# Key products, query products, context sums and the output projection take new places among the attention's steps

## The chip, the cores and the metric

The kernel runs on one core of a Trainium2 chip. The metric is device time in microseconds (us) of one execution. TensorE is called PE here, VectorE DVE, ScalarE ACT, GpSimd POOL and SyncE SP, as in the profile.

## The reference

Three layers follow each other on 4 sequences of 256 tokens with 256 features: half a mixture-of-experts layer, an attention layer, and the same mixture-of-experts layer again, each on layer-normalised input and added to it.

```python
x = x + 0.5 * ffn(layernorm(x))
x = x + attn(layernorm(x))      # the layer that the change is in
x = x + 0.5 * ffn(layernorm(x))

def attn(inputs, w_q, w_k, w_v, w_o, b_o):       # 16 heads of 16 features, t = 256
    q, k, v = ((inputs @ w.T).reshape(b, t, 16, 16) for w in (w_q, w_k, w_v))
    scores = einsum("bqhd,bkhd->bhqk", q, k)     # causal
    attn = softmax(where(causal, -inf, scores) / sqrt(t))
    ctx = einsum("bhqk,bkhd->bqhd", attn, v).reshape(b, t, 256)
    return ctx @ w_o.T + b_o
```

## The kernel before

The feed-forward layers are not touched. Only the attention is of interest, some 120 us between them.

**Steps.** A sequence (`b`, 0 to 3; called a batch) has 8 head pairs, and `sweep` runs 8 steps for each, s = 0 to 7, then 5 more at the end (b = 4, only old work). Every engine runs its own `step(b, old, new)` in program order, and semaphores tie the engines together. The scores of a pair are made `SLAG` = 2 steps after the batch's step 0, so the last two pairs of a batch are scored in steps 0 and 1 of the next. A pair's scores are a "tail" (second 128 queries by 256 keys, bank 0 or 1) and a "head" (first 128 queries by 128 keys, bank 2 or 3).

**A plain step.** PE: `scores` tail, `scores` head, then `weigh` of the pair three steps back. `scores` needs the pair's masked keys from POOL (`mask_keys`, four operations on `k_head`, which has two slots) and, for its bank, DVE's `low` of two pairs before. DVE: tail maximum (L1200), `low` tail of the previous pair (L1214), head maximum (L1204), `low` head (L1214). ACT: `high` of the previous pair (L834, L837), tail exponentials (two L812, each with a read of the accumulator), head exponentials (two L819). When `low` head is done, SP starts the transposition of the pair's probabilities by DMA into `pT` (L446), and `weigh` (L1596 to L1598) of two steps later on waits for it.

**Extra work in some steps.** `chunk(b, c)` makes 128 of the 256 columns of query and of key with 8 matmul records (L1547) in bank 7: query in its left half, key in its right. It stands in steps 0 and 3 (`CHUNK_STEP`), on PE between tail and head scores. ACT copies it out rounded (`k_hi` L798, `q_hi` L799, which shares the memory named xT_hi), between tail and head exponentials. DVE makes the remainders (`k_lo` L1187, `q_lo` L1189) between head maximum and `low` head. The masks of steps 2 to 5 use key chunk 0, those of steps 6, 7 and the next 0, 1 use key chunk 1.

Step 5 (`SUM_STEP`): DVE's `add_up` waits for all weighing of the batch before, reduces banks 5 and 6 to `ctxv` (L1222 twice) and takes the reciprocal (L1224), all ahead of its tail maximum. PE's `weigh` of step 5 writes the same two banks anew, so it waits for both reductions:

```python
if s == SLAG + 3:
    if old:
        pe.wait_ge(ctx_summed, b * 2)
```

Step 6 (`OUT_STEP`): POOL divides `ctxv` (L388, after its masks of step 6); PE transposes it into bank 7 (L1610) between tail and head scores; ACT copies it out as `ctxT` (L844, stored in the memory named wv) ahead of its `high`. Step 7: PE projects (`project_out`, L1617, 8 matmul records, bank 7) ahead of its tail scores, and DVE adds the result to x (`add_attention`, L1229) at the end of the step. `chunk` of the next step 0 waits for that (`attn_added`).

Of the kernel before, what the change touches and what calls it, by code (L numbers as in the profile page):

```python
# [56 lines left out]
P_SCALE = 2.0 ** 15  # L57
VBANK = (3, 4, 5, 6, 5, 6, 5, 6)
VALUES = {1: (0, 2), 2: (2, 4), 3: (4, 6), 4: (6, 8)}
# [4 lines left out]
OBANK = (7, 4)  # L64
CHUNK_STEP = (0, 3)
SUM_STEP, OUT_STEP = 5, 6
# [13 lines left out]
def build(nc, x_in, wq_in, wk_in, wv_in, wo_in, bo_in, wr_in, win_in, wout_in, bias_in, out):  # L80
    with ExitStack() as ctx:
# [241 lines left out]
        v_ready = sem("v_ready")  # L323
        qk_done = sem("qk_done")
        qk_hi_ready = sem("qk_hi_ready")
        k_hi_ready = sem("k_hi_ready")
        k_lo_ready = sem("k_lo_ready")
        qk_ready = sem("qk_ready")
        k_head_ready = sem("k_head_ready")
# [49 lines left out]
        def steps_of(new):  # L379

            return range(HPAIRS if new else SUM_STEP)

# [264 lines left out]
        def _(act):  # L647
# [145 lines left out]

            def chunk(b, c):

                act.wait_ge(qk_done, b * DK + (c + 1))
                reach(act, head_scored, b * HPAIRS + (CPAIRS * (c + 1) - HPAIRS))
                act.activation(k_hi[:, c, :], bank[7][:, SEQ:2 * SEQ], ACT.Copy).then_inc(k_hi_ready, 1)  # L798
                act.activation(q_hi[c][:, :, :], bank[7][:, 0:SEQ].rearrange("p (q t) -> p q t", q=2), ACT.Copy,  # L799
                               scale=1.0 / SEQ ** 0.5).then_inc(qk_hi_ready, 1)  # L800

# [37 lines left out]

            def step(b, old, new):  # L840
                for s in steps_of(new):
                    if old and s == OUT_STEP:
                        act.wait_ge(ctxT_done, b)
                        act.activation(ctxT[:, :, :], bank[7][:, :].rearrange("p (k t) -> p k t", k=DK), ACT.Copy,  # L844
                                       scale=1.0 / P_SCALE).then_inc(ctxT_ready, 1)
                    if old if s < SLAG + 1 else new:
                        high(b, s)
                    if old if s < SLAG else new:
                        exps(b, s, True)
                    if not old and s == 0:  # L850
                        turn_out(1, (1,))
                    if new and s in CHUNK_STEP:
                        chunk(b, CHUNK_STEP.index(s))
# [36 lines left out]
        def _(dve):  # L890
# [292 lines left out]

            def chunk(b, c):

                dve.wait_ge(qk_hi_ready, b * DK + (c + 1))
                dve.tensor_tensor(k_lo[:, c, :], bank[7][:, SEQ:2 * SEQ], k_hi[:, c, :].bitcast(F32), ALU.subtract)\  # L1187
                    .then_inc(k_lo_ready, 1)
                dve.scalar_tensor_tensor(q_lo[c][:, :, :], bank[7][:, 0:SEQ].rearrange("p (q t) -> p q t", q=2),  # L1189
                                         1.0 / SEQ ** 0.5, q_hi[c][:, :, :].bitcast(F32),  # L1190
                                         ALU.mult, ALU.subtract).then_inc(qk_ready, 1)

# [23 lines left out]

            def add_up(b):

                sums = row_sum[:, bass.ds(b - 1, 1), :, :].rearrange("p o q h -> p (o q) h")
                dve.wait_ge(pv_done, b * HEADS)  # L1220
                for qt in range(2):
                    dve.tensor_reduce(ctxv[:, qt, :, :], bank[5 + qt][:, :].rearrange("p (h w d) -> p h d w", w=2, d=HD),  # L1222
                                      AX_X, ALU.add).then_inc(ctx_summed, 1)
                dve.reciprocal(inv_sum[:, :, :], sums).then_inc(inv_ready, 1)  # L1224

            def add_attention(b):
                dve.wait_ge(o_done, b)
                rows = x[:, bass.ds(b * 2 - 2, 2), :]
                dve.tensor_tensor(rows, rows, bank[7][:, :].rearrange("p (q d) -> p q d", q=2), ALU.add)\  # L1229
                    .then_inc(attn_added, 1)  # L1230
# [17 lines left out]
            def step(b, old, new):  # L1248
                for s in steps_of(new):
                    if old and s == SUM_STEP:  # L1250
                        add_up(b)
                    if old if s < SLAG else new:
                        maxima(b, s, True)
                    if old if s < SLAG + 1 else new:
                        low(b, s, True)
                    if old if s < SLAG else new:
                        maxima(b, s, False)
                    if new and s in CHUNK_STEP:
                        chunk(b, CHUNK_STEP.index(s))
# [65 lines left out]
        def _(pe):  # L1325
# [211 lines left out]

            def chunk(b, c):

                if c:  # L1540
                    pe.wait_ge(qk_ready, b * DK + c)
                else:

                    reach(pe, attn_added, b)
                for w, to in ((wq, 0), (wk, SEQ)):
                    for k in range(DK):
                        last = pe.matmul(bank[7][:, to:to + SEQ], w[:, k, c * P:(c + 1) * P], xnT[:, k, bass.ds(b * SEQ, SEQ)],  # L1547
                                         start=(k == 0), stop=(k == DK - 1))
                last.then_inc(qk_done, 1)

            def values(first, last):
                for t in range(first, last):

                    reach(pe, v_rest_ready, t - 1 if t >= 4 else 0)
                    for k in range(DK):
# [4 lines left out]
            def scores(b, s, tail):  # L1560
# [5 lines left out]
                if tail:  # L1566
                    if (s - SLAG) % CPAIRS == 0:

                        pe.wait_ge(qk_ready, b * DK + (c + 1 - (DK if s < SLAG else 0)))
                    pe.wait_ge(k_head_ready, g + 1)  # L1570
# [13 lines left out]
            def weigh(b, s):  # L1584

                g = b * HPAIRS + (s - SLAG - 3)
                ago = s < SLAG + 3
                turned = pT[(s - 1) % 2]
                pe.wait_ge(pT_ready[g % 2], g // 2 * 16 + 16)
# [11 lines left out]
            def turn_context(b, new):  # L1601

                pe.wait_ge(ctx_ready, b)
                if new:

                    pe.wait_ge(qk_ready, b * DK + DK)
                for c in range(DK):
                    for qt in range(2):
                        heads = ctxv[:, qt, c * HPC:(c + 1) * HPC, :].rearrange("p h d -> p (h d)")
                        last = pe.transpose(bank[7][:, c * SEQ + qt * P:c * SEQ + (qt + 1) * P], heads, ident[:, :])  # L1610
                last.then_inc(ctxT_done, 1)

            def project_out(b):
                pe.wait_ge(ctxT_ready, b)
                for qt in range(2):
                    for c in range(DK):
                        last = pe.matmul(bank[7][:, qt * D:(qt + 1) * D], ctxT[:, c, qt * P:(qt + 1) * P], wo[:, c, :],  # L1617
                                         start=(c == 0), stop=(c == DK - 1))
                last.then_inc(o_done, 1)

            def step(b, old, new):
                for s in steps_of(new):
                    if old and s == OUT_STEP + 1:
                        project_out(b)
                    if old if s < SLAG else new:
# [9 lines left out]
                    if new and s in CHUNK_STEP:  # L1635
                        chunk(b, CHUNK_STEP.index(s))
                    if not old and s == SLAG + 1:
# [4 lines left out]
                    if old if s < SLAG + 3 else new:  # L1642
                        if s == SLAG + 3:
# [84 lines left out]
```

## Time and profile before

| | |
|---|---|
| time, median of 3 runs | 421.43 us (420.86 to 422.84) |
| the profiled execution | 420.87 us, its span 419.1 us |
| mean granted TensorE clock | 0.990 |
| busy share of the span | PE 91%, DVE 71%, ACT 61%, POOL 57% |
| step 0 of batch 1 to step 0 of batch 4 | 77.69 us, in three batches of 25.02, 25.40 and 27.27 us |

The span runs from the first to the last instruction; 1.8 us of the profiled execution lie around it. Busy shares are means over stages with different limits, so the attention has to be read by itself. There the start of each tail maximum (DVE L1200) is a clock of the steps: exactly one begins in every step.

### The profile page before, as it was taken

To read this page: it belongs to the slowest core of one execution; us is meant where nothing else is said; L and a number is where in the kernel's file an instruction comes from. 1 tells how busy PE (TensorE), PEld (TensorE's weight loads), DVE (VectorE), ACT (ScalarE), POOL (GpSimd) and SP (SyncE) were. 2 spreads that over 40 slices of the span, in tenths; PEclk is the share of its full clock that TensorE was granted. 3 is DMA by queue.
4 is the path that set the end of the run, shared out by engine and by line. 5 is a ranking of instruction groups with operands and counts; after the bars stand their busy time and mean duration, and the time that the engine had idled before them with its cause. 6 is when DMAs were issued, how large, how long until landed. Compare 5 with 4: busy or idle time off the path is not lost.

```text
span 419.1 us, 9185 instructions
## 1 busy us (share of the span) xinstructions
PE 380.4 (91%) x2732; PEld 309.0 (74%) x2733; DVE 296.6 (71%) x620; ACT 256.6 (61%) x640; POOL 237.5 (57%) x307
## 2 busy tenths in 40 slices
PE   7769999999999989788888988797899999999996
PEld 3548888888888867566666766473788888888885
DVE  6878999555666796887777757967466765566566
ACT  2837865656555546799888878621455556555552
POOL 5255445565567359567878668201555545745860
PEclk9999999999999999899999989999999999999999
DMA  7949921112111620466867587819721111112126
GB/s 253 399 125 391 379 97 54 52 38 75 50 50 38 238 77 0 76 114 116 151 117 129 103 108 145 139 20 305 238 96 55 53 62 52 50 50 57 43 96 231
DMA packets 70929, 51.57 MB, mean 123 GB/s; under 512 B 53104, under 2 KB 64624, under 8 KB 70640
## 3 DMA queue, kind: packets, MB, share of 16 engines
q1 hardware_dynamic: 66064, 36.99, 34.3%
q0 software_dynamic: 4544, 12.07, 9.3%
q10 hardware_dynamic: 288, 2.10, 1.3%
q8 instruction: 17, 0.28, 0.3%
q14 instruction: 16, 0.13, 0.1%
HBM read 29.37 MB, written 9.19 MB: 92 GB/s over the span
## 4 chain that ended last, share of the span: by engine, by line
PE 57%; DMA 16%; DVE 15%; issue 4%; ACT 3%; POOL 2%; SPq 1%; DVEq 0%; ACTq 0%; POOLq 0%
PE bank L1408 27%; PE bank L1430 13%; DMA pT<-parts 5%; DMA w_raw<-in_win_t 4%; PE bank L1418 4%; PE bank L1580 3%; DMA pT<-parts_late 3%; PE bank L1547 3%; PE bank L1384 2%; DMA w_out<-y_scratch 2%; DVE x L1097 2%; DMA y_scratch<-arena,scatter_row 2%; DVE neg_max L1200 1%; PE bank L1617 1%; DVE parts L1214 1%
## 5 line engine op out<-in xcount | busy, mean ns | idle before, releaser
L546 POOL DMA_INDIRECT arena<-xn_scratch,gather_row x46 | 49.6, 1078 | 68.1 <-PE bank L1384 46.7
L552 POOL DMA_INDIRECT y_scratch<-arena,scatter_row x42 | 62.5, 1488 | 37.1 <-ACT arena L715 35.3
L1408 PE MATMUL bank<-w_hi,xT_hi 128*128 x184 | 61.7, 416 | 0.4 <-ACT xT_hi L674 0.4
L1058 DVE TENSOR_TENSOR wo_lo<-w_out,wo_hi 128x1024 fp32r<-128x1024 f32 x46 | 56.3, 1224 | 3.8 <-PE bank L1430 2.2
L1063 DVE TENSOR_TENSOR gT_lo<-bank,gT_hi 128x512 fp32r<-128x512 f32 x46 | 31.7, 690 | 38.1 <-ACT gT_hi L689 38.1
L1408 PE MATMUL bank<-w_hi,xT_lo 128*128 x184 | 57.5, 393 | 0.0
L1408 PE MATMUL bank<-w_lo,xT_hi 128*128 x184 | 57.3, 392 | 0.0
L682 ACT ACTIVATE arena<-bank 128x512 f32<-128x512 f32 x46 | 27.6, 599 | 45.6 <-PE bank L1408 45.6
L627 POOL TENSOR_TENSOR k_head<-k_hi,head_mask 128x256 fp32r<-128x256 f32 x64 | 38.7, 626 | 24.3 <-PE bank L1581 24.3
L704 ACT ACTIVATE wo_hi<-w_out 128x1024 fp32r x46 | 48.8, 1061 | 5.1 <-issue 3.0
L1580 PE MATMUL bank<-k_head,xT_hi 128*128 128x256 f32 (+1 forms) x128 | 40.2, 395 | 7.7 <-DVE parts L1214 5.9
L1047 DVE TENSOR_TENSOR xT_lo<-bank,xT_hi 128x256 fp32r<-128x256 f32 x46 | 19.5, 425 | 34.8 <-ACT xT_hi L674 34.4
L1408 PEld LDWEIGHTS bank<-w_lo,xT_hi 128*128 128x128 f32 x184 | 34.5, 188 | 8.1
L1408 PEld LDWEIGHTS bank<-w_hi,xT_lo 128*128 128x128 f32 x184 | 34.5, 188 | 7.9
L715 ACT ACTIVATE arena<-bank 128x256 f32<-128x256 f32 x42 | 16.2, 386 | 37.2 <-PE bank L1430 37.2
L627 POOL TENSOR_TENSOR k_head<-k_lo,head_mask 128x256 fp32r<-128x256 f32 x64 | 38.0, 614 | 0.6 <-DVE k_lo L1187 0.6
L812 ACT ACTIVATE bank<-bank,neg_max 128x256 f32<-128x256 f32 x64 | 28.5, 446 | 12.4 <-DVE neg_max L1200 11.7
L1430 PE MATMUL bank<-wo_hi,gT_hi 128*128 128x256 f32 x184 | 33.0, 301 | 1.4 <-ACT gT_hi L689 1.4
L1329 PE MATMUL bank<-ones 128*128 128x512 f16 x108 | 28.4, 395 | 4.8 <-POOL ident L496 1.8
L1072 DVE TENSOR_TENSOR arena<-arena,bank 128x512 f32<-128x512 f32 x46 | 31.2, 678 | 1.1 <-PE bank L1408 0.9
L1200 DVE TENSOR_REDUCE neg_max<-bank 128x2 f32<-128x512 f32 x32 | 21.9, 684 | 13.0 <-PE bank L1581 13.0
L1430 PE MATMUL bank<-wo_hi,gT_lo 128*128 128x256 f32 x184 | 30.1, 286 | 0.6 <-DVE gT_lo L1063 0.5
(196 smaller groups left out, 915.5 us busy)
## 6 DMA issues: line engine op xcount, KB each, us to landing
w_raw<-in_win_t SPq DMA_DIRECT2D x8, 1024.0 KB, 10.9
w_out<-in_wout_t SPq DMA_DIRECT2D x16, 512.0 KB, 7.6
w_out<-y_scratch SPq DMA_DIRECT2D x8, 512.0 KB, 5.3
xn_scratch<-arena ACTq DMA_DIRECT2D x2, 1024.0 KB, 6.2
x<-in_x SPq DMA_DIRECT2D x4, 256.0 KB, 3.4
out<-x SPq DMA_DIRECT2D x4, 256.0 KB, 2.2
arena<-xn_scratch,gather_row POOLq DMA_INDIRECT x46, 3.4
y_scratch<-arena,scatter_row POOLq DMA_INDIRECT x46, 3.0
```

The costliest lines, as they stand in the source:

```text
L546: pool.indirect_dma_start(out=xb[j % 2][:, :], out_offset=None, in_=xn_dram, in_offset=bass.IndirectOffsetOnAxis(ap=gather_row[:, j:j + 1] ...
L552: pool.indirect_dma_start(out=y_dram, in_=y[j % 2][:, :], in_offset=None, out_offset=bass.IndirectOffsetOnAxis(ap=scatter_row[:, j:j + 1], ...
L627: ins = pool.tensor_tensor(k_head[s % KSLOTS][:, part, hh, :], k[:, c, :].bitcast(F32), head_mask[:, h % HPC:h % HPC + 1].to_broadcast([P, ...
L704: act.activation(wo_hi[u][:, :, :], w_out[:, bass.ds(e, 1), :, :].rearrange("p o c d -> p (o c) d"), ACT.Copy)\
L812: act.activation(keys, keys, ACT.Exp, bias=neg_max[u][:, 1, hh:hh + 1], accum_out=row_sum[:, bass.ds(batch, 1), 1, h:h + 1]).then_inc(tail ...
L1058: dve.tensor_tensor(wo_lo[:, :, :], w_out[:, bass.ds(e, 1), :, :].rearrange("p o c d -> p (o c) d"), wo_hi[u][:, :, :].bitcast(F32), ALU.s ...
L1063: dve.tensor_tensor(gT_lo[:, :, :], bank[4][:, :].rearrange("p (c t) -> p c t", c=HK), gT_hi[:, :, :].bitcast(F32), ALU.subtract).then_inc ...
L1072: dve.tensor_tensor(g[:, :], sa[:, :], bank[2 + u][:, :], ALU.mult).then_inc(g_done, 1)
L1329: pe.matmul(bank[into][:, :], ones[:, :], bc(ones[:, :], 1, [P, 512 // P, P]), start=True, stop=True)
L1408: last = pe.matmul(bank[2 * half + u][:, :], tok[u][:, k, :], wts[:, bass.ds(e, 1), k, half * H:(half + 1) * H], start=(part == 0 and k == ...
L1430: last = pe.matmul(bank[y_bank(j)][:, 0:D], tok[:, c, :], wts[:, c, :], start=(part == 0 and c == 0), stop=(part == 2 and c == HK - 1))
L1580: pe.matmul(to, q[:, 1 if tail else 0, :], keys[:, part, :, 0:width], start=(n == 0), stop=False)
```

## The change

- Query and key get banks of their own (query bank 4, key bank 7) and are made apart: key chunk 0 of the next batch in step 6, query chunk 0 in step 0, key chunk 1 in step 3, query chunk 1 in step 4. In the very first batch key chunk 0 is made in step 0. The last batch has no next one and makes none in step 6.
- The context sum: one of the two reductions stays ahead of step 5's tail maximum, the other goes between `low` tail and head maximum of step 5. The reciprocal goes to the end of step 4.
- The transposition of the context goes behind `weigh` in step 6, its copy on ACT behind the head exponentials; both use bank 4.
- The projection goes in two halves: one between tail and head scores of step 7, one behind its `weigh`.
- The value products of the first batch leave bank 4 (`VBANK`). `weigh` and its wait stay where they are.

```diff
-VBANK = (3, 4, 5, 6, 5, 6, 5, 6)
+VBANK = (3, 5, 6, 5, 6, 5, 6, 5)
-CHUNK_STEP = (0, 3)
+KEY_STEP, QUERY_STEP = (6, 3), (0, 4)
 # ACT, step
-                    if old and s == OUT_STEP:
-                        act.wait_ge(ctxT_done, b)
-                        act.activation(ctxT[:, :, :], bank[7][:, :].rearrange("p (k t) -> p k t", k=DK), ACT.Copy,
-                                       scale=1.0 / P_SCALE).then_inc(ctxT_ready, 1)
                     if old if s < SLAG + 1 else new:
                         high(b, s)
                     if old if s < SLAG else new:
                         exps(b, s, True)
...
+                    if new and s == KEY_STEP[0] and b + 1 < BATCH:
+                        key_chunk(b + 1, 0)
+                    if new and s == KEY_STEP[1]:
+                        key_chunk(b, 1)
+                    if new and s in QUERY_STEP:
+                        query_chunk(b, QUERY_STEP.index(s))
                     if old if s < SLAG else new:
                         exps(b, s, False)
+                    if old and s == OUT_STEP:
+                        act.wait_ge(ctxT_done, b)
+                        act.activation(ctxT[:, :, :], bank[4][:, :].rearrange("p (k t) -> p k t", k=DK), ACT.Copy,
+                                       scale=1.0 / P_SCALE).then_inc(ctxT_ready, 1)
 # DVE, step
-                    if old and s == SUM_STEP:
-                        add_up(b)
+                    if old and new and s == SUM_STEP:
+                        add_up(b, 0)
                     if old if s < SLAG else new:
                         maxima(b, s, True)
                     if old if s < SLAG + 1 else new:
                         low(b, s, True)
+                    if old and new and s == SUM_STEP:
+                        add_up(b, 1)
                     if old if s < SLAG else new:
                         maxima(b, s, False)
...
                     if old if s < SLAG + 1 else new:
                         low(b, s, False)
+                    if old and new and s == SUM_STEP - 1:
+                        invert(b)
 # PE, step
-                    if old and s == OUT_STEP + 1:
-                        project_out(b)
                     if old if s < SLAG else new:
                         scores(b, s, True)
-                    if old and s == OUT_STEP:
-                        turn_context(b, new)
...
+                    if old and new and s == OUT_STEP + 1:
+                        project_out(b, 0)
...
                         weigh(b, s)
+                    if old and new and s == OUT_STEP + 1:
+                        project_out(b, 1)
+                    if old and new and s == OUT_STEP:
+                        turn_context(b, new)
```

The chunk functions are the old one cut in two, with a semaphore for each product; on PE:

```python
def key_chunk(b, c):
    reach(pe, k_lo_ready, b * DK + c)
    ...                                   # 2 matmuls into bank 7, then k_done
def query_chunk(b, c):
    reach(pe, q_ready, b * DK + c)
    if c == 0:
        reach(pe, attn_added, b)
    ...                                   # 2 matmuls into bank 4, then q_done
```

## Rows read from the trace of the kernel before

**Rows 1.** By stretch: us, then PE, PEld, DVE, ACT, POOL busy, clock, DMA, GB/s.
```profile
185.01:210.03 25.02, 21.77 (x236) 16.92 (x234) 18.96 (x40) 21.94 (x86) 19.63 (x35) 1.00 0.71 128
210.03:235.43 25.40, 22.00 (x236) 17.24 (x236) 18.98 (x42) 21.96 (x86) 19.64 (x35) 1.00 0.72 126
235.43:262.70 27.27, 23.35 (x238) 18.38 (x239) 18.97 (x41) 21.96 (x86) 19.62 (x35) 0.94 0.71 117
```

**Rows 2.** Timeline of ACT in batch 2: start, duration, work.
```profile
212.13 0.38 ACT L798 ACTIVATE k_hi<-bank 128x256 fp32r<-128x256 f32 x1 [0.35 <-PE bank L1547]
212.41 0.38 ACT L799 ACTIVATE xT_hi<-bank 128x256 fp32r<-128x256 f32 x1
...
216.32 0.59 ACT L834 ACTIVATE parts<-bank 128x512 f16<-128x512 f32 x1
...
217.23 0.45 ACT L812 ACTIVATE bank<-bank,neg_max 128x256 f32<-128x256 f32 x1
...
218.16 0.34 ACT L819 ACTIVATE bank<-bank,neg_max 128x128 f32<-128x128 f32 x1
...
218.86 0.60 ACT L834 ACTIVATE parts_late<-bank 128x512 f16<-128x512 f32 x1
...
229.33 0.60 ACT L844 ACTIVATE wv<-bank 128x512 f32<-128x512 f32 x1 [0.51 <-PE bank L1610]
```

**Rows 3.** Timeline of DVE in batch 2, steps 0 to 7.
```profile
213.28 0.42 DVE L1189 SCALAR_TENSOR_TENSOR xT_lo<-bank,xT_hi 128x256 fp32r<-128x256 f32 x1
213.62 0.41 DVE L1214 SCALAR_TENSOR_TENSOR parts_late<-bank,parts_late 128x256 f16<-128x256 f32 x1
...
216.50 0.69 DVE L1200 TENSOR_REDUCE neg_max<-bank 128x2 f32<-128x512 f32 x1 [0.58 <-PE bank L1581]
...
217.71 0.41 DVE L1204 TENSOR_REDUCE neg_max<-bank 128x2 f32<-128x256 f32 x1
...
219.55 0.69 DVE L1200 TENSOR_REDUCE neg_max<-bank 128x2 f32<-128x512 f32 x1 [1.09 <-PE bank L1581]
...
223.10 0.69 DVE L1200 TENSOR_REDUCE neg_max<-bank 128x2 f32<-128x512 f32 x1
...
224.97 1.28 DVE L1222 TENSOR_REDUCE ctxv<-bank 128x256 f32<-128x512 f32 x2
226.17 0.34 DVE L1224 RECIPROCAL inv_sum<-placed 128x32 f32<-128x32 f32 x1
226.43 0.63 DVE L1200 TENSOR_REDUCE neg_max<-bank 128x2 f32<-128x512 f32 x1
...
232.89 0.69 DVE L1200 TENSOR_REDUCE neg_max<-bank 128x2 f32<-128x512 f32 x1 [1.09 <-PE bank L1581]
```

**Rows 4.** The chain that ended last, in order of time, at step 2.
```profile
214.06 3.88 DMA pT<-parts_late
```

**Rows 5.** Timeline of PE in batch 2, steps 3, 6 and 7.
```profile
218.44 0.71 PE L1580 MATMUL bank<-k_head,xT_hi 128*128 128x512 f32 x2
...
219.35 1.03 PE L1547 MATMUL bank<-arena,wq 128*128 128x256 f32 x4
220.22 1.03 PE L1547 MATMUL bank<-arena,wk 128*128 128x256 f32 x4
220.89 0.59 PE L1580 MATMUL bank<-k_head,xT_hi 128*128 128x256 f32 x2
...
222.01 0.48 PE L1580 MATMUL bank<-k_head,xT_hi 128*128 128x512 f32 x1
...
230.06 1.97 PE L1617 MATMUL bank<-wo,wv 128*128 128x256 f32 x8
231.69 0.58 PE L1580 MATMUL bank<-k_head,xT_hi 128*128 128x512 f32 x1
```

**Rows 6.** The same columns as rows 1, around step 3 of batch 3.
```profile
242.00:243.00 1.00, 0.33 (x3) 0.10 (x1) 1.00 (x2) 0.96 (x4) 1.00 (x3) 1.00 1.04 194
...
244.00:245.00 1.00, 1.00 (x20) 0.90 (x21) 0.00 (x0) 1.00 (x5) 0.96 (x2) 0.50 0.70 154
```

More of the change, by code:

```diff
@@ L379, in steps_of @@
         def steps_of(new):
-            return range(HPAIRS if new else SUM_STEP)
+            return range(HPAIRS if new else SLAG + 3)
         def divide(eng, b):
@@ L1255, in step @@
                         low(b, s, True)
+                    if old and new and s == SUM_STEP:
+                        add_up(b, 1)
                     if old if s < SLAG else new:
                         maxima(b, s, False)
[L1258 to L1259 removed]
+                    if not old and s == 0:
+                        key_chunk(0, 0)
+                    if new and s == KEY_STEP[0] and b + 1 < BATCH:
+                        key_chunk(b + 1, 0)
+                    if new and s == KEY_STEP[1]:
+                        key_chunk(b, 1)
+                    if new and s in QUERY_STEP:
+                        query_chunk(b, QUERY_STEP.index(s))
                     if old if s < SLAG + 1 else new:
                         low(b, s, False)
+                    if old and new and s == SUM_STEP - 1:
+                        invert(b)
                     if not new and s == 0:
@@ L1536, in _, with key_chunk, query_chunk @@
             pe.wait_ge(xnT_ready, TPAIRS + 1)
[L1538 to L1542, printed above, removed]
-                    reach(pe, attn_added, b)
[L1545 to L1549, printed above, removed]
+            def key_chunk(b, c):
+                reach(pe, k_lo_ready, b * DK + c)
+                for k in range(DK):
+                    last = pe.matmul(bank[7][:, 0:SEQ], wk[:, k, c * P:(c + 1) * P], xnT[:, k, b * SEQ:(b + 1) * SEQ],
+                                     start=(k == 0), stop=(k == DK - 1))
+                last.then_inc(k_done, 1)
+            def query_chunk(b, c):
+                reach(pe, q_ready, b * DK + c)
+                if c == 0:
+                    reach(pe, attn_added, b)
+                for k in range(DK):
+                    last = pe.matmul(bank[4][:, 0:SEQ], wq[:, k, c * P:(c + 1) * P], xnT[:, k, b * SEQ:(b + 1) * SEQ],
+                                     start=(k == 0), stop=(k == DK - 1))
+                last.then_inc(q_done, 1)
             def values(first, last):
                 for t in range(first, last):
-                    reach(pe, v_rest_ready, t - 1 if t >= 4 else 0)
+                    reach(pe, v_rest_ready, t - 1 if t >= 3 else 0)
                     for k in range(DK):
@@ L1609, in turn_context, with project_out @@
                         heads = ctxv[:, qt, c * HPC:(c + 1) * HPC, :].rearrange("p h d -> p (h d)")
-                        last = pe.transpose(bank[7][:, c * SEQ + qt * P:c * SEQ + (qt + 1) * P], heads, ident[:, :])
+                        last = pe.transpose(bank[4][:, c * SEQ + qt * P:c * SEQ + (qt + 1) * P], heads, ident[:, :])
                 last.then_inc(ctxT_done, 1)
-            def project_out(b):
+            def project_out(b, qt):
                 pe.wait_ge(ctxT_ready, b)
[L1615 to L1619, printed above, removed]
+                for c in range(DK):
+                    last = pe.matmul(bank[4][:, qt * D:(qt + 1) * D], ctxT[:, c, qt * P:(qt + 1) * P], wo[:, c, :],
+                                     start=(c == 0), stop=(c == DK - 1))
+                if qt:
+                    last.then_inc(o_done, 1)
             def step(b, old, new):
                 for s in steps_of(new):
-                    if old and s == OUT_STEP + 1:
-                        project_out(b)
                     if old if s < SLAG else new:
@@ L1632, in step @@
                         turn(2, (0,))
-                    if old and s == OUT_STEP:
-                        turn_context(b, new)
-                    if new and s in CHUNK_STEP:
-                        chunk(b, CHUNK_STEP.index(s))
+                    if not old and s == 0:
+                        key_chunk(0, 0)
+                    if new and s == KEY_STEP[0] and b + 1 < BATCH:
+                        key_chunk(b + 1, 0)
+                    if new and s == KEY_STEP[1]:
+                        key_chunk(b, 1)
+                    if new and s in QUERY_STEP:
+                        query_chunk(b, QUERY_STEP.index(s))
+                    if old and new and s == OUT_STEP + 1:
+                        project_out(b, 0)
                     if not old and s == SLAG + 1:
```

58 lines of the change are left out of this document (32 added, 26 removed).

## Prediction

> **What bounds the kernel now.** I read the busy time of each engine by stretch first. A batch of attention takes 25.02, 25.40 and 27.27 us, and ACT is busy for 21.94 to 21.96 us of each, DVE for 19, POOL for 19.6 [rows 1]. PE's 22 us are partly pipeline. So no engine is full: at most 25.40 - 21.96 = 3.4 us a batch is waiting, some 10 us over three batches, and that is all that a new order could win.
>
> The timelines come next, with the start of each tail maximum as T. ACT without a gap needs 0.91 us for two `high` copies, 0.93 for the tail and 0.70 for the head exponentials, 2.54 us a step [rows 2]. Step 2 starts at 216.50, step 3 at 219.55, step 4 at 223.10, step 5 at 226.43, step 7 at 232.89 [rows 3], and batch 2 itself runs from 210.03 to 235.43 [rows 1]. Against 2.54 a step, steps 0 to 3 take 9.52 for 7.62, step 3 to 4 3.55, step 4 to 5 3.33, and steps 5 to 0 take 9.00 for 7.62. The reader should see that each loss stands beside an extra job: chunk, sum, projection.
>
> The chain tells what the chunk of step 0 does. `low` head of step 0 starts at 213.62, 3.59 us after T0 [rows 3]. Its transposition lands at 214.06 + 3.88 = 217.94 [rows 4], `weigh` of step 2 waits for it, and T3 comes 1.61 later. So from a late `low` head to the tail maximum three steps on it is 4.32 + 1.61 = 5.93 us. In a plain step `low` head starts 1.21 + 0.33 = 1.54 after T (217.71 less 216.50, and the 0.34 between two such operations), and 1.54 + 5.93 = 7.47 hides under ACT's 7.62: the two are nearly tied.
>
> **Prices used.** From T to the tail exponentials 0.73 (217.23 less 216.50); a hand-over between engines 0.04 (the maximum ends at 217.19, ACT starts at 217.23); one rounded copy costs ACT 0.28 and takes 0.38 [rows 2, 3]. A remainder costs DVE 0.34, `low` head 0.34, a reduction 0.60 to the next and 0.68 to its end (1.28 less 0.60), the reciprocal 0.26 [rows 3]. On PE: tail scores 0.91 up to a product, 1.11 up to T; one product 0.87 when first and 0.67 when second; head scores and `weigh` together 1.12 (220.89 to 222.01); the projection 1.63, so 0.82 a half; tail scores behind a projection 1.20 up to T (231.69 to 232.89) [rows 3, 5].
>
> **The change, part by part, in a batch.**
>
> *Steps 0 to 3.* PE holds one product instead of two, but what is late now is the remainder of the query: it waits for ACT's copy, which stands behind the tail exponentials. `low` head starts at 0.73 + 0.93 + 0.38 + 0.04 + 0.34 = 2.42 after T0 instead of 3.59. T3 = 2.42 + 5.93 = 8.35 instead of 9.52: 1.17 won. ACT alone would allow 7.62 + 0.28 = 7.90.
>
> *Step 3 to 4.* PE: 0.91 + 0.87 + 1.12 = 2.90; DVE 2.42 + 0.34 = 2.76; ACT 2.54 + 0.28 = 2.82. PE ends last: 2.90 instead of 3.55, 0.65 won. With the product at 0.67 it is ACT's 2.82.
>
> *Step 4 to 5.* Before, step 4 had no chunk. Now DVE waits for the query's rounded copy, so `low` head starts at 2.42, ends its turn at 2.76, then the reciprocal 0.26 and the first reduction 0.60: 3.62 instead of 3.33, 0.29 lost. Behind DVE's wait stand the reduction and the maximum, and ACT waits for the latter.
>
> *Step 5 to 6.* `weigh` still waits for both reductions, and the second has been put behind the tail maximum. It starts at T5 + 1.21, ends at 1.89, and after `weigh` and the tail scores T6 is at 1.89 + 1.61 = 3.50. This is the cost that moving half the sum does not show by itself: before, both reductions were over ahead of T5 and hid under DVE's own time. Behind the waiting `weigh` on PE stand the tail scores of step 6, and everything waits for these.
>
> *Step 6 to the next 0.* The copy of the context stands behind the head exponentials: 0.73 + 0.93 + 0.28 + 0.70 = 2.64 after T6. It takes 0.60, and PE's projection follows 0.13 later (229.93 to 230.06), at 3.37 [rows 2, 5]. First half 0.82, head scores and `weigh` 1.12, second half 0.82, then 1.20 to the tail maximum: 3.37 + 0.82 + 1.12 + 0.82 + 1.20 = 7.33. The tail scores of step 7 fit in the wait ahead of the first half. Cutting the projection in two removes no PE work; its second half stands squarely ahead of the next step's tail scores. Steps 5 to 0 so take 3.50 + 7.33 = 10.83 instead of 9.00: 1.83 lost. The second half starts at T6 + 5.31 and is over at about 6.3; adding the attention to x (512 columns on DVE, 0.69 as the tail maximum of the same size) ends at about 7.0, before T0, and the query product, due at 6.13 + 0.91 = 7.04, does not wait for it.
>
> *At no cost.* POOL's 32 mask and 2 divide operations of a batch take 19.64 us [rows 1], 0.58 each. The two divides can only start at T5 + 1.9 and take some 1.2; the mask of step 7 then ends at about T5 + 5.4 (four operations, 2.3 us), and PE wants it at T6 + 2.1 = T5 + 5.6. It is covered by 0.2 us; without the cover, each 0.1 late is 0.1 on T7. The number of transpositions and SP's order don't change. The key chunk of step 6 is ready long before masks need it.
>
> *Sum of a batch.* 8.35 + 2.90 + 3.62 + 3.50 + 7.33 = 25.70, against 25.02, 25.40 and, in batch 3, 25.40 plus a clock dip of 1.87. Batch 3 has no key chunk in step 6 and takes 25.42. So +0.68, +0.30, +0.02: +1.0 us. Batch 0 gives one copy (0.28) out of step 3 and takes one into step 4 and one into step 6: +0.3, with value work around it that can hide or double this (0 to 0.6). Together +1.3 us on 420.87 = 422.2. This execution is 0.56 under the median of 421.43, so I forecast 422.7. The unknown bounds (product 0.67 or 0.87, ties between engines of 0.1 to 0.2 a step) make it 0.3 us a batch either way, 421.5 to 424.
>
> **TensorE's clock.** In batch 3, PE had 0.33 us of work in one us, then little, and at 244 the granted clock was 0.50 (1.2 GHz) while PE was fully busy with what had waited [rows 6]. That stretch cost 27.27 - 25.40 = 1.87 us. I read it as the wait of `weigh` on a late transposition, since step 0 has its chunk in this batch too. The changed kernel has a wait of that kind in each batch: head scores of step 5 can start when `low` head of step 4 is done, at T5 - 0.86, and take less than the 1.12 that they need with `weigh`. So PE has no work from T5 + 0.3 at the latest to T5 + 1.9, for 1.6 to 2.7 us.
>
> The Trainium skill ("TensorE: Matmul & The Clock Gate", section "HAM oscillation") warns that gaps in which the matmul engine idles between bursts bring its clock down, so that the burst behind each gap runs slow. By that rule, if it struck in every batch, the sum would be 422.7 + 2 x 1.87 = 426.4. The trace agrees as far as rows 6 go; that batches 1 and 2 kept full clock shows it doesn't strike every time.
>
> **The rivals.**
>
> *A, one dip more or three dips instead of one.* For it: the new wait in step 5. Against it: before, similar waits in other batches left the clock at 1.00 [rows 1]. One more is 424.6, two more 426.4. Chance 0.30 in all, 0.20 and 0.10.
>
> *B, the dip of batch 3 goes.* The late transposition that led to it is 1.17 earlier. Then 422.7 - 1.9 = 420.8. Chance 0.15.
>
> *C, faster.* One mechanism: PE's held `weigh` in step 5 doesn't pace steps 5 to 0, ACT does. It decides at the point where `weigh` can start by T5 + 1.66, when ACT ends the tail exponentials. Then these steps take 3 x 2.54 + 0.28 for the key copy + 0.60 for the context's = 8.50 instead of 10.83, and the kernel 422.7 - 3 x 2.33 = 415.7. For it: ACT has the most work of the three others [rows 1]. Against: the wait stays in the code and its end is DVE's, T5 + 1.89 at the earliest. Chance 0.10, half of it only part of the way, around 418.5.
>
> *D, the change does less than it says.* POOL's masks wait for free slots rather than for keys, and wins and losses shrink together: 421.4, chance 0.05.
>
> My forecast itself has 0.40.
>
> **How the numbers follow.** No change that can be measured here is within 0.5% (419.3 to 423.5). It gets D and B, and of the forecast three quarters (its part up to 423.5): 0.05 + 0.15 + 0.30 = 0.50. Slower gets A and the rest of the forecast: 0.30 + 0.10 = 0.40. Faster is C, 0.10. The range goes from 419.3, which leaves most of C out, to 426.0, which leaves the last tenth of A out. The forecast's own range is 421.5 to 424.
>
> **What the new profile would show.** `low` head of step 0 some 2.4 us after the tail maximum, not 3.6; steps 0 to 3 in about 8.4 us. The tail maximum of step 5 3.6 after that of step 4. In step 5, the second reduction behind the first `low`, PE idle until it ends, and 3.5 us to step 6. Between the halves of the projection no long wait, and 7.3 us from step 6 to the next step 0. ACT busy for 22 us a batch as before. I am wrong if `weigh` of step 5 is not the one that PE waits on, if batches take under 25.2 us at full clock, or if the clock falls more than once after step 0 of batch 1.

## The result and the profile after

The changed kernel takes 424.05 us, median of 10 runs (421.92 to 425.06), against 421.45 for the kernel before (10 runs, 419.69 to 422.84). The ratio is 1.0071, with a 95% interval of 1.0048 to 1.0094: 0.7% slower. The profiled execution took 424.78 us, its span 423.0 us against 419.1, its mean granted clock 0.976 against 0.990. Of the kernels built later, both_whole and sum_alone had three runs each over 1.5% above their fastest; the ratios, medians and low-clock times below leave those out, and the profile of both_whole is one of them.

The stretches of batches 1, 2 and 3 come first, from tail maximum to tail maximum of step 0, with the columns of [rows 1].

```profile
188.18:214.84 26.66, 23.12 (x236) 17.77 (x235) 19.49 (x40) 22.43 (x87) 19.89 (x35) 0.94 0.68 122
214.84:240.99 26.15, 23.01 (x236) 18.20 (x237) 19.58 (x40) 21.99 (x85) 19.71 (x35) 0.93 0.67 122
240.99:266.55 25.56, 21.02 (x234) 16.54 (x235) 19.16 (x39) 21.50 (x84) 19.68 (x35) 1.00 0.68 125
```

The loss of this one execution adds up over the span. Up to the first tail maximum it is 0.41 us (161.75 for 161.34), in batch 0 (to its successor's step 0) 2.76 (26.43 for 23.67), in batch 1 1.64, in batch 2 0.75, in batch 3 a gain of 1.71, and behind it 0.05 (156.45 for 156.40): 3.90, the difference of the spans. The clock column matters: batches 1 and 2 now run partly at half speed (0.94 and 0.93), and batch 3, which did so before, no longer does. In batch 0 the clock is 0.87 on average, against 0.93 before.

DVE's timeline of batch 2, with L1216 the tail maximum, L1206 the query's remainder, L1238 the reciprocal and L1243 the two reductions, answers to [rows 3]:

```profile
214.84 0.69 DVE L1216 TENSOR_REDUCE neg_max<-bank 128x2 f32<-128x512 f32 x1
...
217.24 0.41 DVE L1230 SCALAR_TENSOR_TENSOR parts_late<-bank,parts_late 128x256 f16<-128x256 f32 x1
...
223.01 0.69 DVE L1216 TENSOR_REDUCE neg_max<-bank 128x2 f32<-128x512 f32 x1 [0.69 <-PE bank L1617]
...
225.74 0.68 DVE L1216 TENSOR_REDUCE neg_max<-bank 128x2 f32<-128x512 f32 x1
...
227.79 0.42 DVE L1206 SCALAR_TENSOR_TENSOR xT_lo<-bank,xT_hi 128x256 fp32r<-128x256 f32 x1 [0.30 <-ACT xT_hi L805]
...
228.46 0.34 DVE L1238 RECIPROCAL inv_sum<-placed 128x32 f32<-128x32 f32 x1
228.72 0.63 DVE L1243 TENSOR_REDUCE ctxv<-bank 128x256 f32<-128x512 f32 x1
229.26 0.68 DVE L1216 TENSOR_REDUCE neg_max<-bank 128x2 f32<-128x512 f32 x1
...
230.45 0.68 DVE L1243 TENSOR_REDUCE ctxv<-bank 128x256 f32<-128x512 f32 x1
...
232.76 0.69 DVE L1216 TENSOR_REDUCE neg_max<-bank 128x2 f32<-128x512 f32 x1 [0.96 <-PE bank L1617]
```

`low` head of step 0 starts 2.40 us after the tail maximum instead of 3.59, and steps 0 to 3 take 8.17 instead of 9.52. Step 3 to 4 takes 2.73 instead of 3.55. In step 4 DVE waits 0.30 for ACT's query copy, and step 4 to 5 takes 3.52 instead of 3.33. The second reduction ends at 230.45 + 0.68 = 231.13, and step 5 to 6 takes 3.50 instead of 2.47.

The waits of the same stretch name it on PE (total, times, longest), once for its weights and once for its matmuls:

```profile
PEld bank L1632 <- DVE ctxv L1243: 2.0, 1, 2.0
PE bank L1632 <- DVE ctxv L1243: 1.9, 1, 1.9
```

And the stretches around that wait, with the clock as the first number behind POOL:

```profile
228.00:231.00 3.00, 1.12 (x7) 0.60 (x5) 3.00 (x7) 2.23 (x9) 1.44 (x3) 1.00 0.80 154
231.00:234.00 3.00, 2.81 (x27) 2.21 (x28) 2.04 (x5) 2.08 (x9) 2.72 (x5) 0.81 0.57 108
234.00:237.00 3.00, 3.00 (x31) 2.52 (x29) 1.14 (x4) 2.12 (x10) 2.63 (x6) 0.62 0.36 67
```

PE works 1.12 of 3 us, then has everything to do that had waited, and does part of it at half speed: 2.4 falls to 1.2 GHz. To be set beside [rows 5], from PE's timeline: the one key product of step 6, four records, takes 1.62 us there; four such records took 1.03.

```profile
232.56 1.62 PE L1572 MATMUL bank<-arena,wk 128*128 128x256 f32 x4
```

### The profile page after: what moved, and what is told of

It is laid out like the page before. It is cut to its first block, busy times and chain, and to the rows that moved or that the text cites. A ratio compares the mean times of both kernels' runs of the same rounds, so it can differ in the third digit from the quotient of the medians.

```text
span 423.0 us, 9196 instructions
## 1 busy us (share of the span) xinstructions
PE 386.1 (91%) x2732; PEld 312.0 (74%) x2733; DVE 298.7 (71%) x620; ACT 256.6 (61%) x640; POOL 237.2 (56%) x307
## 4 chain that ended last, share of the span: by engine, by line
PE 64%; DVE 15%; DMA 8%; issue 6%; ACT 5%; POOL 2%; DVEq 1%; ACTq 0%; SPq 0%; POOLq 0%
PE bank L1438 27%; PE bank L1460 13%; PE bank L1616 4%; PE bank L1448 4%; PE bank L1359 3%; DMA pT<-parts 3%; PE bank L1414 2%; ACT bank L818 2%; DVE w_lo L942 2%; DMA arena<-xn_scratch,gather_row 2%; DVE neg_max L1216 2%; DMA w_out<-y_scratch 2%; PE bank L1652 1%; DVE v L1314 1%; DVE parts L1230 1%
## 5 line engine op out<-in xcount | busy, mean ns | idle before, releaser
L1616 PE MATMUL bank<-k_head,xT_hi 128*128 128x256 f32 (+1 forms) x128 | 42.7, 416 | 8.4 <-DVE parts L1230 6.3
L1359 PE MATMUL bank<-ones 128*128 128x512 f16 x108 | 32.1, 436 | 3.5 <-POOL ident L497 1.8
L1216 DVE TENSOR_REDUCE neg_max<-bank 128x2 f32<-128x512 f32 x32 | 22.0, 687 | 14.5 <-PE bank L1617 14.1
L1616 PEld LDWEIGHTS bank<-k_head,xT_hi 128*128 128x128 f32 x128 | 22.3, 201 | 12.8 <-issue 7.5
```

Of the source, the lines that this page charges most:

```text
L1359: pe.matmul(bank[into][:, :], ones[:, :], bc(ones[:, :], 1, [P, 512 // P, P]), start=True, stop=True)
L1616: pe.matmul(to, q[:, 1 if tail else 0, :], keys[:, part, :, 0:width], start=(n == 0), stop=False)
```

## The experiments

All were compared with the kernel before on the same chip. Beside the ratio, two readings are used. The first is the distance between tail maxima in one profile. The second is the low-clock time of a run: a run of span s and mean granted clock c has 2 x (1 - c) x s us at half clock. For the 84 runs of the kernel before that came with the experiments it is 9.4 us on average; for the 10 runs of the changed kernel 17.3. In the profiles this time comes in low stretches of 3.4 us each, or of 6.8.

| kernel | median, us | ratio (95%) | low clock, us | steps 0-3, 3-5, 5-6, 6-0 in batch 2 |
|---|---|---|---|---|
| before | 421.4 to 421.6 | 1 | 9.4 | 9.52, 6.88, 2.47, 6.53 |
| changed | 424.05 | 1.0071 (1.0048 to 1.0094) | 17.3 | 8.17, 6.25, 3.50, 8.23 |
| sum_whole | 422.43 | 1.0021 (0.9990 to 1.0052) | 12.8 | 8.15, 6.84, 2.52, 7.13 |
| out_whole | 425.77 | 1.0125 (1.0082 to 1.0168) | 23.1 | 8.20, 6.25, 3.49, 7.43 |
| both_whole | 422.00 | 0.9996 (0.9966 to 1.0027) | 12.3 | 8.20, 6.84, 2.77, 8.79 |
| filled | 425.25 | 1.0077 (1.0048 to 1.0106) | 13.0 | 8.32, 6.25, 3.49, 7.13 |
| sum_query_early | 418.40 | 0.9933 (0.9906 to 0.9959) | 10.0 | 8.28, 5.98, 2.92, 7.12 |
| filled_all | 430.92 | 1.0248 (1.0215 to 1.0280) | 23.5 | 10.28, 7.41, 3.50, 7.13 |
| before_filled | 431.33 | 1.0237 (1.0191 to 1.0284) | 18.3 | 11.81, 7.46, 2.46, 6.65 |
| sum_query_filled | 421.36 | 1.0015 (0.9989 to 1.0041) | 9.6 | 9.62, 5.98, 2.91, 7.14 |
| sum_alone | 424.03 | 1.0065 (1.0027 to 1.0102) | 14.5 | 9.51, 6.24, 3.49, 6.57 |
| out_alone | 421.04 | 1.0002 (0.9979 to 1.0025) | 7.4 | 9.34, 6.88, 2.46, 6.87 |
| first_query_3 | 423.82 | 1.0061 (1.0029 to 1.0093) | 19.4 | 8.23, 6.25, 3.69, 8.27 |
| best_first_3 | 418.78 | 0.9928 (0.9900 to 0.9957) | 11.5 | 8.25, 5.97, 2.88, 7.13 |

**One part undone: sum_whole.**

```diff
 # DVE, step of the changed kernel
                     if old and new and s == SUM_STEP:
                         add_up(b, 0)
+                        add_up(b, 1)
                     if old if s < SLAG else new:
                         maxima(b, s, True)
                     if old if s < SLAG + 1 else new:
                         low(b, s, True)
-                    if old and new and s == SUM_STEP:
-                        add_up(b, 1)
```

> The changed kernel, but both reductions of the context sum stand ahead of the tail maximum of step 5 again (the reciprocal stays at the end of step 4). Theory 1, the held weighing is the cost: steps 4 to 5 grow from 3.52 by one reduction, 0.60, to 4.12; steps 5 to 6 fall from 3.50 to ACT's 2.54; 0.36 us less a batch at full clock, the wait of PE in step 5 is gone, and with it at least one of the two clock dips after step 5 (about 1 us each): 421.5 to 423. Theory 2, the divided projection and the late context copy are the cost: steps 6 to 0 stay at 6.9 to 8.2 and the time stays at 424. Theory 3, the clock is all of it: the same gain as theory 1 at the clock, none where the clock was full.

Batches 1 and 2 ran at a clock of 1.00 in its profile (batch 3 had a low stretch in steps 2 and 3, as in the kernel before, and took 26.50):

```profile
188.37:213.15 24.78, 21.68 (x236) 16.82 (x235) 19.59 (x40) 22.06 (x87) 20.32 (x36) 1.00 0.73 133
213.15:237.79 24.64, 21.86 (x236) 17.12 (x237) 19.70 (x41) 21.52 (x85) 19.68 (x35) 1.00 0.77 128
```

Step 4 to 5 took 4.11, step 5 to 6 2.52: as theory 1 had it, to 0.02 us. The low-clock time of its runs is 4.5 us less than the changed kernel's. The time is 1.6 us less, and no longer to be told from the kernel before. Steps 6 to 0 also fell, from 8.23 to 7.13, which speaks against theory 2: their length in the changed kernel was partly the clock's. By order alone, batches 1 and 2 are 0.36 and 0.55 us shorter than the same batches of filled below, which are the changed kernel's at full clock.

**The output part undone: out_whole, and both undone: both_whole.**

```diff
 # ACT, step of the changed kernel: the copy of the context ahead of high() again
 # PE, step
+                    if old and new and s == OUT_STEP + 1:
+                        project_out(b, 0)
+                        project_out(b, 1)
                     if old if s < SLAG else new:
                         scores(b, s, True)
+                    if old and new and s == OUT_STEP:
+                        turn_context(b, new)
...
-                        project_out(b, 0)     # and project_out(b, 1), turn_context(b, new) behind weigh
 # both_whole: this and the edit of sum_whole
```

> The changed kernel, but the output part is as before, in bank 4: context transposed between tail and head scores of step 6, its copy ahead of the rounded copies, the whole projection ahead of the tail scores of step 7. Theory 1: worked out with the key product still in step 6, steps 6 to 7 are 3.99 (before) + 0.87 = 4.86 and 7 to 0 2.54, together 7.40 against 7.33 worked out for the changed kernel, so nothing is won; the held weighing of step 5 stays at 3.50: 424 within 0.7. Theory 2, the divided projection is the cost: steps 6 to 0 fall to 6.53, 0.8 a batch: 421.6.

> Sum and output part both as before; what is left of the change is that keys and queries are made apart (steps 6, 3 and 0, 4) and the reciprocal at the end of step 4. Theory 1: 8.2 + 2.73 + 4.12 + 2.54 + 7.40 = 25.0 us a batch, 24.1 in the last one, against 25.0, 25.4 and 25.4 before: 1.7 us less than before at equal clock, 419.7. Theory 2 (divided projection the cost): lower than the kernel with the whole sum by 0.8 a batch, 418. Rival: the products' new places are no gain at all, then it is at 421 or above.

With the projection whole, steps 6 to 0 take 7.43 in batch 2, against 7.40 expected, so theory 2 falls: dividing it was not the loss. The whole time is 1.7 us above the changed kernel and its low-clock time is the highest but one; the wait of step 5 is still in it. both_whole was expected at 419.7 and came out at 422.00. Its last batch, at full clock, took 24.18 (24.1 expected), but batches 1 and 2 took 26.54 and 26.60 with steps 6 to 0 at 8.1 and 8.8, against 7.4 at full clock. At full clock the order of work gave what it should; in this one profile the clock took it back. Its low stretches begin some 1 and 2 us behind the tail maximum of step 5, where this kernel has no held weighing, so that wait is not the only thing that goes before a low stretch there.

**PE kept at work in the wait: filled.**

```diff
 # PE, step of the changed kernel, s == 5, ahead of the wait on ctx_summed
+                            if old:
+                                for _ in range(14):
+                                    pe.matmul(bank[7][:, SEQ:2 * SEQ], ones[:, :], bc(ones[:, :], 1, [P, 2, P]), start=True,
+                                              stop=True)
```

> The changed kernel with 14 idle-time products of 256 columns (ones by ones, into the unused half of bank 7) on PE in step 5, between head scores and the held weighing, some 1.5 of the 2.0 us that PE waits there; no result depends on them. Theory 3, the clock dips come from this wait: batches 1 and 2 keep a clock of 1.00 and fall from 26.66 and 26.15 to 25.3 to 25.7: 421.5 to 422.5. Theory 1: steps 5 to 6 stay at 3.50 all the same. If the dips have another cause, the time stays at 424 or rises by what the products delay.

In the profile, the products stand in the wait, and batches 1 to 3 keep the full clock:

```profile
227.38 1.69 PE L1686 MATMUL bank<-ones 128*128 128x256 f16 x14
```

```profile
187.76:212.90 25.14, 23.14 (x250) 18.08 (x249) 19.56 (x40) 22.25 (x87) 20.32 (x36) 1.00 0.78 132
212.90:238.09 25.19, 23.34 (x250) 18.35 (x251) 19.65 (x41) 21.70 (x85) 19.68 (x35) 1.00 0.76 127
238.09:263.62 25.53, 22.52 (x248) 17.81 (x249) 19.15 (x39) 21.50 (x84) 19.68 (x35) 1.00 0.74 125
```

This is the cleanest sight of the change without its clock: 25.14, 25.19 and 25.53, together 75.86 us. The kernel before without its one dip is 25.02 + 25.40 + 25.40 = 75.82. Steps 5 to 6 stay at 3.49. As a whole the kernel did not gain, though: 425.25. In the profile, time was lost elsewhere (from step 0 of the last, old-only steps to the end it has 160.5 us for 156.4, with two low stretches). The runs have 4.3 us less of low clock than those of the changed kernel and are still 1.2 us longer. So filled shows the local cost and not a remedy, and holding the clock here did not make the kernel faster.

**More such products, and a control: filled_all, before_filled, sum_query_filled.** The same loops of 256-column products, in the first batch ahead of the tail scores of steps 4 and 6 as well (20 and 10; 8 and 8; 12 and 10), and in before_filled 8 in step 5. In filled_all and sum_query_filled the loops of the first batch stand behind a wait for the query's remainder.

> The changed kernel with the idle-time products in step 5 of each later batch (14), and also in the first batch ahead of the tail scores of step 4 (20) and of step 6 (10), where PE waited 3.5 and 1.75 us; no result depends on them. Clock theory: the first batch falls from 26.4 (T2 to the next T0) to about 24 and the mean number of 3.4 us stretches at the lower clock from 5.1 to 3 or less; 421.5. If the low stretches only move elsewhere, 424 stays. Order-of-work theory: no change but through the clock.

> The kernel before with the same kind of products, 8 in each of the three places (its waits there are 1.1 us), in bank 4. A control: if such products help by the clock, this kernel, which spends only 2.6 such stretches at the lower clock, gains at most 1 us: 420.5 to 421.5. If they cost time by themselves it shows here, above 422.

> The kernel with whole sum and early query, with idle-time products in the first batch only (12 ahead of step 4, 10 ahead of step 6). Both theories together: 420 less one to two low stretches of 1.2 us, 418 to 419, which beats the kernel before (421.4). If the low stretches move elsewhere, as without them.

The control missed by 10 us and filled_all by 9, so the products are no clean test of the whole time. In before_filled it is steps 2 to 3, in which there are none, that grow to 5.35 us from 3.05. The chain of waits shows the same transposition as [rows 4], step 0 of batch 2, 5.34 us to landing instead of 3.88:

```profile
218.05 5.34 DMA pT<-parts_late
...
223.44 0.21 PE bank L1596
```

Batches 1 to 3 of it ran at 0.94 of the clock on average. sum_query_filled, which is sum_query_early with 22 such products, is 3 us above that kernel at the same low-clock time (9.6 for 10.0 us): there the kernel lost time without the clock. Its steps 2 to 3 in batches 1 and 2 take 4.12 and 4.11 us instead of 3.03 and 2.78, at a clock of 1.00 and with no added product in them. The chain shows the same transposition:

```profile
215.19 5.18 DMA pT<-parts_late
```

That added matmuls go with a slow transposition elsewhere is taken up at the end. For the first batch these kernels are of use all the same, as there they ran at full clock: filled_all has the changed kernel's order and before_filled the old one.

```profile
161.03:185.50 24.47, 21.86 (x169) 17.04 (x168) 19.98 (x40) 18.95 (x75) 17.54 (x26) 1.00 0.42 60
161.72:185.63 23.91, 19.50 (x151) 14.79 (x150) 19.50 (x38) 18.74 (x74) 17.82 (x27) 1.00 0.39 67
```

The new order costs the first batch 0.56 us. With one low stretch at 179 to 181 us it is 25.40 to 25.45 (filled, sum_whole, out_whole) against 24.73 and 24.76 for the old order (sum_alone, out_alone): 0.6 to 0.7. The kernel before, whose program for the first batch is that of sum_alone and out_alone, took 1.1 us less than they did, 23.67, with its low stretch at 172 us.

**Each part alone, on the kernel before: sum_alone, out_alone.** The first is the change to `add_up` and `invert` with nothing else, the second the new places of context transposition, copy and half projections, all in bank 7.

> The kernel before with one part of the change alone: one reduction ahead of step 5's tail maximum, the other behind the first `low`, the reciprocal at the end of step 4. Theory 1 (the held weighing costs more than the earlier maximum gives): steps 4 to 5 fall from 3.33 to 2.73, steps 5 to 6 grow from 2.47 to 3.50; 0.43 a batch, 1.3 in all, and more low-clock stretches on top: 422.7 to 424. Rival: splitting the sum is neutral and the loss seen was that of the query product in step 4: 421.4.

> The kernel before with another part alone: context transposed behind `weigh` in step 6, its copy behind the head exponentials, the projection in two halves in step 7, all in bank 7. By the prediction's working, steps 6 to 0 take 0.73 + 0.93 + 0.70 + 0.73 + 0.82 + 1.12 + 0.82 + 1.20 = 7.05 (6.87 where the changed kernel ran at full clock without key product) instead of 6.53: 0.34 to 0.52 a batch, 422.5 to 423. Rival: the divided projection pays: 420 or less.

DVE's timeline of batch 2 in sum_alone, steps 4, 5 and 6:

```profile
225.96 0.69 DVE L1200 TENSOR_REDUCE neg_max<-bank 128x2 f32<-128x512 f32 x1
...
228.63 0.68 DVE L1200 TENSOR_REDUCE neg_max<-bank 128x2 f32<-128x512 f32 x1
...
229.82 0.68 DVE L1227 TENSOR_REDUCE ctxv<-bank 128x256 f32<-128x512 f32 x1
...
232.12 0.69 DVE L1200 TENSOR_REDUCE neg_max<-bank 128x2 f32<-128x512 f32 x1 [0.96 <-PE bank L1589]
```

2.67 and 3.49 where 2.73 and 3.50 stood in the expectation; batches 1 and 2 are 0.40 and 0.41 longer. Over three batches that is 1.2 us of order. The kernel is 0.65% slower, 2.7 us, and its low-clock time is 14.5 us for 9.4. This one part alone gives the slowdown of the whole change; at the price per us worked out in the next section, half of it or somewhat more goes with the clock. The profile does not show how: its low stretches in the span stand at 14, 27 and 181 us, in the feed-forward layer and the first batch, and none of its three waits of step 5 is followed by one. In out_alone, steps 6 to 0 take 6.87 in every batch, the 0.34 more that was allowed for, with the clock at 1.00:

```profile
185.37:210.71 25.34, 22.02 (x237) 17.00 (x235) 19.16 (x40) 22.61 (x87) 19.77 (x35) 1.00 0.74 128
210.71:236.26 25.55, 22.23 (x237) 17.22 (x237) 19.17 (x40) 21.94 (x85) 19.60 (x35) 1.00 0.70 125
236.26:262.38 26.12, 22.24 (x238) 17.37 (x239) 19.16 (x40) 21.93 (x85) 19.60 (x35) 1.00 0.73 122
```

Its time is that of the kernel before, where 422.5 to 423 was expected, and its low-clock time the lowest of all, 7.4 us. PE's work of step 7 lies more evenly there; that this is why is argued, not shown.

**The query's second product elsewhere: sum_query_early, first_query_3, best_first_3.**

```diff
 # sum_query_early: sum_whole and
-KEY_STEP, QUERY_STEP = (6, 3), (0, 4)
+KEY_STEP, QUERY_STEP = (6, 3), (0, 2)
 # first_query_3 (on the changed kernel) and best_first_3 (on sum_query_early), PE, ACT and DVE
-                    if new and s in QUERY_STEP:
-                        query_chunk(b, QUERY_STEP.index(s))
+                    if new and s in ((0, 3) if not old else QUERY_STEP):
+                        query_chunk(b, 1 if s else 0)
```

> The kernel with the whole sum ahead of step 5's tail maximum, and the query's second product in step 2 instead of 4. Theory 1 (order of work): `low` head of step 4 no longer waits for the query's copy, so steps 4 to 5 fall from 4.11 to the 3.33 of the kernel before; full-clock batches fall from 24.7 to 23.9, the kernel from 422.4 to about 420. Rival: the query's remainder now delays `low` head of step 2, and by the transposition the tail maximum of step 5: 8.35 after T2, which 2.6 + 2.7 + 3.3 = 8.7 just covers; if it does not, the gain is half.

> The changed kernel, but in the first batch the query's second product is made in step 3 beside the key's, as in the kernel before. If its place in step 4 lengthened the first batch (T2 to the next T0 took 26.4, 25.4 without the second low-clock stretch, and 23.7 before), this goes back to some 24.0, with step 4 to 5 at 4.1 instead of 4.78, and the time to 422.5. If not, 424.

> The fastest kernel so far (whole sum, query's second product in step 2) with the same return to step 3 in the first batch only. The first batch took 25.8 there; at 24.0 the kernel is at 416.7 instead of 418.4.

sum_query_early is 0.67% faster than the kernel before, 1.6 us better than the 420 expected. Its batches 1 and 2 are, with those of best_first_3 (23.90 and 24.23), the shortest of all:

```profile
188.69:212.61 23.92, 21.86 (x236) 16.92 (x235) 19.63 (x41) 22.07 (x87) 20.33 (x36) 1.00 0.73 138
212.61:236.91 24.30, 21.77 (x236) 17.04 (x237) 19.67 (x40) 21.53 (x85) 19.69 (x35) 1.00 0.77 128
236.91:261.60 24.69, 21.43 (x234) 16.61 (x235) 19.41 (x40) 21.27 (x84) 19.66 (x35) 1.00 0.78 133
```

Step 4 to 5 takes 3.25, as nothing stands ahead of the sum but `low` head. ACT is busy for 22 of 23.9 us: little is left to win by order.

In first_query_3 the first batch did fall, to 23.95, but not where the product was moved: steps 3 to 5 take 5.05 and 4.52, together 9.57 for 9.56 (4.1 was expected for the second), and the gain is in steps 5 to 7, 2.53 and 2.72 for 3.32 and 4.41. Its low stretch stands at 173 us, as in the kernel before, and steps 5 to 7 are free of it; in filled_all, with the product still in step 4 and no low stretch, they take 2.53 and 3.27. The time of the whole kernel stayed (423.82 where 422.5 was expected, low-clock time 19.4). In the profile of best_first_3 the low stretch is back at 181 us, the first batch took 25.64, with steps 5 to 7 at 3.07 and 3.77, and its time is that of sum_query_early, not the 416.7 expected. So most of what the place of the product seemed to cost in the first batch was the place of a low stretch.

## Why the prediction was right

The forecast was 422.7 with a range of 419.3 to 426.0; 424.05 is inside the range, 1.35 above the forecast, on the side (slower) that had 0.40 of the chance, and just outside the forecast's own 421.5 to 424. Of its three signs of being wrong one stayed out, as `weigh` of step 5 is what PE waits on. The other two came: batches took under 25.2 us at full clock (25.14 and 25.19 in filled), and the clock fell three times behind step 0 of batch 1 (at 205, 233 and 287 us). The steps one by one:

- *The bound.* Confirmed: ACT's busy time of a batch is 21.3 to 22.6 us in all kernels, and the order decides what is added to it.
- *Steps 0 to 3*: 8.35 forecast, 8.17 to 8.32 measured in batches 1 and 2 (changed kernel and filled), but 8.94 and 8.93 in batch 3, at full clock too. *Step 3 to 4*: 2.90 and 2.73; the product costs PE 0.7 rather than 0.87, the lower bound. *Step 4 to 5*: 3.62 and 3.52.
- *The held weighing*: 3.50 forecast, 3.50 measured, 3.49 at full clock in filled, 3.50 in sum_alone. The mechanism and its size are shown by undoing it and by doing it alone.
- *Steps 6 to 0*: 7.33 forecast, 7.13 at full clock (filled, sum_whole), 0.34 more than before in out_alone. The copy of the context stands where the forecast had it and starts at 236.47, the first half of the projection at 237.13. PE waits for it at full clock only (filled, 0.6 us in all); in batch 2 of the changed kernel its tail scores, at half clock, end later.
- *Sum of a batch*: 25.70 forecast, 25.14 and 25.19 measured in filled, and 25.53 in batch 3, where 25.42 was forecast. The term over all three batches was +1.0; at full clock it is 75.86 - 75.82 = 0. In batches 1 and 2 it was mis-sized by small errors of one sign.
- *Batch 0*: +0.3 forecast (0 to 0.6), 0.56 by order (filled_all against before_filled). The profile's +2.76 is mostly the clock: behind a PE wait of 1.75 us the low stretch lasts 7 us instead of 3.4 and stands on steps 5 to 7.
- *The clock*, +0 in the forecast: this is the size that was wrong. Runs of the changed kernel spend 7.9 us more at half clock than those of the kernel before. Over the 84 runs before, a run is 0.25 us longer for each us at half clock (correlation 0.70), over the 10 of the changed kernel 0.35 (0.84). By these prices 2.0 to 2.7 of the 2.6 us are the clock's. That is an estimate from the spread of the runs, not shown by an experiment that changes the clock alone. With the 0.6 us of order it makes 2.6 to 3.3. Rival A, to which I gave 0.30, is what happened, but at another price: I took 1.87 us for a low stretch, and 3.4 us at 0.25 to 0.35 are 0.9 to 1.2. The 1.87 held a late transposition as well, 4.41 us to landing instead of 3.88. Rival B happened with it: the dip of batch 3 went, and others came.

Two errors thus cancelled in part, 0.7 us too much for order and some 2 us too little for the clock; that the time fell so near the forecast is in part luck. Rival C is refuted in its condition, `weigh` starting by T5 + 1.66: it starts at T5 + 1.92 or 1.93 in all batches of the six kernels with the divided sum. The Trainium skill's warning ("TensorE: Matmul & The Clock Gate", section "HAM oscillation"), which I used as a rival, agrees in direction: the wait is followed by half clock in batches 1 and 2 of the changed kernel, though it is shorter than the gaps in the Trainium skill's example, and the runs of sum_whole, without the wait, spend 4.5 us less at half clock. Had I taken it as likely in each batch, I would have forecast 426.4, 2.4 us off on the other side.

Over all profiles, a low stretch begins within 4 us of the tail maximum of step 5 in 7 of the 12 batches with the held weighing, in none of the 6 in which products fill that wait, and in 2 of the 24 with the sum whole, both in both_whole. What stays open is why some waits of 1 to 2 us go before a low stretch and others of the same size do not (batch 3 of the changed kernel and all three batches of sum_alone have the wait of step 5 and a clock of 1.00), and why low stretches in the feed-forward layer ahead, which the change does not touch, come and go with the kernel (none in the kernel before, two in sum_alone).

## What to carry to other kernels

Splitting a job so that its second half comes later helps only if nobody waits for the whole of it; look for the wait on the last of its signals before cutting it, and move that or leave the job whole. Price a new TensorE wait twice: its length, and the work behind it that may run at half clock. Before a difference of one stretch between two profiles is called an effect of the order, look where the low stretches lie in both. When the product of a rounded pair is moved, its cost is where the remainder stands in the queue of the engine that has something else to hand on: here, with the sum left whole, taking the query product out of the step of the sum turned a ratio of 1.0021 into 0.9933.

## What the hardware showed that was not expected

The transfers that the profile's page calls "instruction" (in q8, 17 packets of 16 KB in the kernel before, and in q14, smaller ones) coincide with slow transpositions. In the packet records of the 14 kernels, a transposition that stands by itself takes 2.0 us from its first packet to its last where no q8 packet is under way (median of 212, longest 2.54), and 2.5 where one is (median of 63, longest 3.34). In the attention the q8 packets come every 11 to 17 us. A transposition delayed so reaches `weigh` late. The wait ahead of the low clock in batch 3 of the kernel before [rows 6] had a smaller one, 8 KB in q14 at 242.68 us, and the transposition behind it took 4.41 us to landing.

The added products of before_filled and filled_all lengthen PE's program, and steps 2 to 3 of their batches, where no product had been added, took 4.42 to 5.35 us, against 3.05 and 3.07 in batches of the kernel before at full clock. In sum_query_filled they took 4.11 and 4.12 with no low clock. There the q8 packets come at 193.25 and 218.56 us, each in the midst of the transpositions that the tail maximum of step 3 comes after; in sum_query_early, without the 22 products, they come at 196.73 and 220.61, when the packets of these transpositions are over or within 0.2 us of their end. That the longer program moves the packets onto the transpositions that matter is the likely link; no run was made to separate it, and part of the growth in before_filled and filled_all is the clock's.
